# A mixture-of-experts layer that starts its blocks when two of four batches' rows are scattered, not three, with its routing work reordered

## What is computed

```python
x = x + 0.5 * _L0_ffn_ref(_layernorm(x, axis=-1), ln_g, ln_b, router_w, eg, eb, W1, b1, W2, b2, Wo, bo)
x = x + _L0_attn_ref(_layernorm(x, axis=-1), W_qkv, W_o)
x = x + 0.5 * _L0_ffn_ref(_layernorm(x, axis=-1), ln_g, ln_b, router_w, eg, eb, W1, b1, W2, b2, Wo, bo)
```

```python
xf = _layernorm(x.reshape(-1, Dd), ln_g, ln_b)
scores, idx = jax.lax.top_k(xf @ router_w, K)
gate = jax.nn.softmax(scores, axis=-1)
# one expert, for the rows that chose it
x = _layernorm(xf, g, b)
hidden = (x @ W1 + b1) * silu(clip(x @ W2 + b2))
out = out + gate * (hidden @ Wo + bo)
```

## Time and profile before

| | |
|---|---|
| time, median of 3 runs | 1293.15 us (1292.27 to 1294.56) |
| the profiled execution's own time | 1283.73 us |
| its span, and mean granted TensorE clock | 1282.0 us, 0.981 |
| busy: PE, DVE, ACT, POOL | 1144.8, 1124.8, 878.0, 518.6 us |
| the routing, to the first product of the mixture | up to 105 us |
| first mixture, attention, second mixture | from there to about 330, to about 1035, to the end |

### The profile page before, as it was taken

One profiled execution on the slowest core, in us unless ns is written; L12 is line 12 of the kernel. 1 busy time (PEld: TensorE's weight loads), 2 busy tenths in 40 slices (PEclk: granted clock), 3 DMA queues, 4 the chain that ended last, 5 costly groups with the idle time before them and its releaser, 6 DMA issues.

```text
span 1282.0 us, 27027 instructions
## 1 busy us (share of the span) xinstructions
PE 1144.8 (89%) x9003; PEld 606.4 (47%) x9003; DVE 1124.8 (88%) x2287; ACT 878.0 (68%) x1849; POOL 518.6 (40%) x672
## 2 busy tenths in 40 slices
PE   3857999888699999999999999999999999999993
PEld 2745888877322222332223223222222367788882
DVE  7877888887799999989999999999999778988885
ACT  1223555555289999898889888898887965455651
POOL 3883556424224001525336333445344128543232
PEclk9999999999689999999999999999999999999997
DMA  8115565563110200012011000010000413555653
GB/s 278 53 63 181 206 204 194 196 238 137 51 51 18 68 18 4 16 31 55 2 31 37 21 18 18 20 42 10 18 9 25 147 72 142 193 206 191 243 200 141
DMA packets 58746, 123.28 MB, mean 96 GB/s; under 512 B 12736, under 2 KB 33954, under 8 KB 58576
## 3 DMA queue, kind: packets, MB, share of 16 engines
q1 hardware_dynamic: 49616, 103.57, 23.6%
q0 software_dynamic: 8704, 16.93, 4.2%
q10 hardware_dynamic: 288, 1.05, 0.2%
HBM read 36.39 MB, written 23.62 MB: 47 GB/s over the span
## 4 chain that ended last, share of the span: by engine, by line
PE 59%; DVE 25%; POOL 6%; issue 5%; DMA 3%; ACT 2%; SPq 1%; DVEq 0%; POOLq 0%; ACTq 0%
PE psum L2329 15%; DVE att_neg_part L1996 13%; PE psum L2301 9%; PE psum L2232 8%; PE psum L2220 7%; PE psum L2222 7%; PE psum L2283 6%; POOL rows_dram L1293 4%; DVE ffn_x2c L1938 2%; DMA ffn_block_rows<-rows_dram 2%; DVE ffn_hidden L1949 2%; DVE stats L1631 1%; PE psum L2307 1%; ACT ffn_silu L1454 1%; PE psum L2172 1%
## 5 line engine op out<-in xcount | busy, mean ns | idle before, releaser
L1996 DVE TENSOR_REDUCE att_neg_part<-psum 128x2 f32<-128x1024 f32 x512 | 594.7, 1215 | 27.0 <-PE psum L2283 24.9
L1486 ACT ACTIVATE att_probs<-psum 128x512 f32<-128x512 f32 x1024 | 556.4, 597 | 59.8 <-PE psum L2301 23.0
L2329 PE MATMUL psum<-att_probs,att_values 128*18 128x256 f32 x4096 | 322.2, 387 | 4.3 <-issue 3.7
L2283 PE MATMUL psum<-att_right,att_left 62*128 62x512 f16 x1024 | 288.1, 391 | 31.0 <-DVE att_neg_part L1996 30.1
L1454 ACT ACTIVATE ffn_silu<-ffn_x2c,ffn_rec 128x256 f32<-128x256 f32 (+1 forms) x320 | 154.7, 487 | 170.4 <-DVE ffn_x2c L1938 169.9
L1309 POOL DMA_INDIRECT y_dram<-ffn_y,ffn_block_rows x144 | 142.6, 990 | 233.9 <-ACT ffn_y L1472 205.5
L2301 PE MATMUL psum<-att_right,att_left 64*128 64x512 f16 x512 | 199.0, 389 | 0.1
L2307 PE MATMUL psum<-att_right,att_left 64*128 64x512 f16 x512 | 194.9, 381 | 0.0
L1938 DVE TENSOR_SCALAR ffn_x2c<-psum,ffn_rec 128x256 f32<-128x256 f32 (+1 forms) x320 | 162.6, 512 | 34.0 <-PE psum L2222 29.7
L2220 PE MATMUL psum<-ffn_block_t,ffn_rec 128*128 128x256 f32 (+1 forms) x640 | 178.7, 361 | 1.8 <-ACT ffn_block_t L1405 1.8
L2222 PE MATMUL psum<-ffn_block_t,ffn_rec 128*128 128x256 f32 (+1 forms) x640 | 178.0, 360 | 0.0
(11 more groups left out here) (236 smaller groups left out, 1040.8 us busy)
## 6 DMA issues: line engine op xcount, KB each, us to landing
ffn_rec<-record SPq DMA_DIRECT2D x80, 776.5 KB, 3.8
ffn_block_rows<-rows_dram SPq DMA_DIRECT2D x64, 130.0 KB, 3.1
record<-in_L_ffn_W SPq DMA_DIRECT2D x16, 256.0 KB, 6.4
att_left<-q_parts_dram SPq DMA_DIRECT2D x64, 64.0 KB, 2.2
att_right<-att_max_parts SPq DMA_DIRECT2D x256, 1.0 KB
y_dram<-ffn_y,ffn_block_rows POOLq DMA_INDIRECT x144, 2.3
x_sb<-in_L_attn_x SPq DMA_DIRECT2D x4, 512.0 KB, 7.1
record<-in_L_ffn_Wo SPq DMA_DIRECT2D x8, 256.0 KB, 7.2
```

What stands on the lines that cost most here:

```text
L1486: S.activation(probs[:, slot % PROBS, :], ring_bank(("score", slot))[:, :], ACT.Exp, scale=unlift).then_inc(att_bank.by_act, 1)
L1996: V.tensor_reduce(out=neg_part[:, h % 2, keys, p::PAIR, t], in_=psum[:, low:high + 1, :], axis=AX.X, op=ALU.max, negate=True).then_inc(red ...
L2283: product = TE.matmul(bank[max_banks(n)[k]], left[s][PRODUCTS[k], p, q], right[s][PRODUCTS[k], p, seen], start=True, stop=True)
L2329: last = TE.matmul(value_bank[g * VS:g * VS + 2 * VW, p * HALF // 2:(p + 1) * HALF // 2], values_flat[:, at:at + 2 * VW], queries, start=( ...
```

## The change

Six things change, all of them in the first 170 us or so.

1. SP, DVE and ACT start the mixture when the rows of batches 0 and 1 are scattered. The first `AHEAD` = 9 blocks are full ones that two batches fill in any case: `vector_lay_out_early` lists them first, by the new counts `rows_ahead`. SP waits for the rows of batch 2 ahead of block 9. Batch 2's 16 scatters follow behind batch 1's on POOL, and batch 3's 16 all go into `HEAD`.
2. The late layout, nine pieces of DVE work, goes from ahead of the mixture into `HEAD`: one piece ahead of chunk 2 of each of the blocks 2 to 10. SP's eight loads of filler rows move from blocks 8 to 15 to blocks 14 to 16.
3. The rows to be sent out are made by ACT (`scalar_fill`, from a new `offset`), no longer by DVE at step 6. For batch 3 ACT does it in four pieces in `HEAD`, ahead of chunks 1, 2 and 3 of block 1 and chunk 0 of block 2.
4. The list of the routing is written anew: the first norm of a batch (L1660, 8 instructions of DVE) goes from step 0 to step 2, which for batch 1 is behind the places of batch 0; the `fold` passes of PE and ACT go to other places, ACT's behind each batch's exponential and rows.
5. PE may transpose the first half of `xf` when that half is ready, and the PSUM banks of the routing are two shared pairs and no longer one bank for each batch.
6. The scaling of the attention's weights (`scalar_lift`, two instructions of ACT) moves from ahead of the mixture to ahead of chunk 0 of block 3, and the constants of DVE wait for one POOL instruction fewer.

The diff, cut to what the text speaks of (renamed helpers and split semaphores are left out):

```diff
+    AHEAD = -((E * (BLOCK - 1) - TOPK * N * (B - 2)) // BLOCK)
...
-        route_bank = [Banks([bank[b]], semaphore(f"route_full{b}"), semaphore(f"route_emptied{b}"))
-                      for b in range(B)]
+        route_banks = [Banks(bank[2 * k:2 * k + 2], semaphore(f"route_full{k}"), semaphore(f"route_emptied{k}"))
+                       for k in range(2)]
+        route_bank = [route_banks[b % 2] for b in range(B)]
...
-        FIRST_OUT = 2
+        OUT_SLOTS = [0, 2, 4, 6, 8, 10, 12, 14, 16, 18, 20, 24, 28, 32, 36, 40]
         for block in range(BEGIN, BEGIN + 3):
             plan_head(block, [(0, "turned", block, 0)])
-        for n in range(FIRST_OUT, BT * TOPK):
-            HEAD[HC * (n - FIRST_OUT)].append(("route", JOBS[B - 1], ROUTE_STEPS - 1, (n, BT * TOPK)))
+        for n in range(BT * TOPK):
+            HEAD[OUT_SLOTS[n]].append(("route", JOBS[B - 1], ROUTE_STEPS - 1, (n, BT * TOPK)))
+        for n in range(9):
+            HEAD[HC * (1 + n) + 2].append(("lay", 1, 0, (n, 9)))
+        for n in range(4):
+            HEAD[n + 1].append(("fill", B - 1, 0, (n, 4)))
+        HEAD[HC * 2].append(("lift", 0, 0, WHOLE))
...
+            def each(what, pieces):
                 for n in pieces:
-                    if n <= E:
-                        yield "fold", n, 0, WHOLE
+                    yield what, n, 0, WHOLE
+            def scatter(b, places):
+                for n in places:
+                    yield "route", JOBS[b], SCATTER, (n, BT * TOPK)
+            yield "constants", 0, 0, WHOLE
             yield from steps(0, range(6))
             yield from steps(1, (0,))
             yield from steps(0, (6,))
+            yield "fill", 0, 0, (0, 2)
+            yield "fold", 0, 0, WHOLE
+            yield "scale", 0, 0, WHOLE
             yield from steps(1, (1,))
-            yield from steps(0, range(7, SCATTER))
-            yield from folds((0,))
-            for b in range(1, B):
-                yield from steps(b, (2,))
-                yield from folds((3 * b - 2,))
-                yield from scatters(b - 1, 0)
-                yield from steps(b, (3, 4))
-                yield from scatters(b - 1, 1)
-                yield from steps(b, (5,))
-                yield from folds((3 * b - 1, 3 * b))
-                yield from steps(b + 1, (0,))
-                yield from steps(b, (6,))
-                yield from scatters(b - 1, 2)
-                yield from steps(b + 1, (1,))
-                yield from steps(b, (7,))
-                yield from scatters(b - 1, 3)
-                yield from steps(b, (8, 9))
-                if b == B - 1:
-                    yield "folded", 0, 0, WHOLE
-                yield from scatters(b - 1, 4)
-                yield from steps(b, (10, 11))
-                if b == B - 2:
-                    yield "lay", 0, 0, WHOLE
-                yield from scatters(b - 1, 5)
+            yield from steps(0, (7, 8, 9, 10))
+            yield "fill", 0, 0, (1, 2)
+            yield from steps(0, (11,))
+            yield "square", 0, 0, WHOLE
+            yield from each("fold", (1, 2))
+            yield from each("scale", (1, 2))
+            yield from steps(1, (2, 3, 4))
+            yield from scatter(0, range(0, 5))
+            yield from steps(1, (5,))
+            yield "fold", 3, 0, WHOLE
+            yield from steps(2, (0,))
+            yield from steps(1, (7, 8, 9, 6))
+            yield from scatter(0, range(5, 7))
+            yield from each("fold", (4, 5))
+            yield from steps(2, (1,))
+            yield from steps(1, (10,))
+            yield "fill", 1, 0, WHOLE
+            yield from steps(1, (11,))
+            yield from each("scale", (3, 4, 5))
+            yield from scatter(0, range(7, 13))
+            yield from steps(2, (2, 3, 4, 5))
+            yield "fold", 6, 0, WHOLE
+            yield from steps(3, (0,))
+            yield from steps(2, (7, 8, 9, 6))
+            yield from each("fold", (7, 8))
+            yield from scatter(0, range(13, 15))
+            yield from steps(3, (1,))
+            yield from scatter(0, range(15, 16))
+            yield from steps(2, (10,))
+            yield "fill", 2, 0, WHOLE
+            yield from steps(2, (11,))
+            yield from each("scale", (6, 7, 8))
+            yield "lay", 0, 0, WHOLE
+            yield "norm", 0, 0, WHOLE
+            yield "folded", 0, 0, WHOLE
+            yield from scatter(1, range(0, 16))
+            yield from steps(3, (2, 3, 4, 5))
+            yield from steps(3, (7, 8, 9, 6, 10, 11))
+            yield "lifts", 0, 0, WHOLE
+            yield from scatter(2, range(0, 16))
...
-                for job in JOBS[0:B - 1]:
+                for job in JOBS[0:B - 2]:
...
+            if k == 0 and i == AHEAD:
+                sync_rows_written(JOBS[B - 2])
...
-            for n in range(FIRST_OUT):
-                pool_route(JOBS[B - 1], ROUTE_STEPS - 1, (n, BT * TOPK))
...
+                if k_ffn == 0:
+                    G.wait_ge(*rows_by_act(job))
...
+        def scalar_fill(b, part):
+            job, r = JOBS[b], sets[b]
+            S.wait_ge(*by_dve(job, FILLED))
+            for t in share(part, BT):
+                last = S.activation(r.rows[:, t, :, 0:F], r.xf[:, t, :].unsqueeze(1).to_broadcast([P, TOPK, F]),
+                                    ACT.Identity, bias=r.offset[:, t:t + 1], scale=r.rstd[:, t:t + 1])
+            if last_of(part):
+                last.then_inc(r.by_act, 1)
...
-                S.wait_ge(lifts_made, 1)
-                S.activation(wqkv_t[:, :], wqkv_t[:, :], ACT.Copy, scale=lifts[:, 0:1].bitcast(F32))
-                S.activation(wo_t[:, :], wo_t[:, :], ACT.Copy, scale=lifts[:, 1:2].bitcast(F32)).then_inc(lifted, 1)
...
+        def scalar_lift():
+            S.wait_ge(lifts_made, 1)
+            S.activation(wqkv_t[:, :], wqkv_t[:, :], ACT.Copy, scale=lifts[:, 0:1].bitcast(F32))
+            S.activation(wo_t[:, :], wo_t[:, :], ACT.Copy, scale=lifts[:, 1:2].bitcast(F32)).then_inc(lifted, 1)
...
-            vector_lay_out_late()
...
+                    if t == nt // 2 - 1 and k_ffn == 0:
+                        last.then_inc(r.by_dve, 1)
...
+                if k_ffn == 0:
+                    V.scalar_tensor_tensor(r.offset[:, :], r.mean_var[:, :, 0], -1.0, r.rstd[:, :],
+                                           ALU.mult, ALU.mult).then_inc(r.by_dve, 1)
+                    return
...
+            if k_ffn == 0 and b == B - 3:
+                V.tensor_tensor(rows_ahead[:, :], carry[0:1, :], region[0:1, :], ALU.subtract)
...
-                    settle(V.tensor_scalar(firsts_f[:, :], first_rows[:, :], float(BLOCK - 1), None, ALU.add))
-                    settle(V.tensor_copy(firsts_i[:, :], firsts_f[:, :]))
+                    if ahead:
+                        settle(V.tensor_copy(firsts_i[:, :], ahead[:, :]))
+                    else:
+                        settle(V.tensor_scalar(firsts_f[:, :], first_rows[:, :], float(BLOCK - 1), None, ALU.add))
+                        settle(V.tensor_copy(firsts_i[:, :], firsts_f[:, :]))
```

More of the change, by code:

```diff
@@ L304, in build_macaron @@
         powers_i = sbuf("powers_i", [P, 3], I32, first)
-        sets.extend(RouteSet(k, first) for k in range(1, B - 1))
+        sets.extend(RouteSet(k, first) for k in range(1, B - 2))
+        first.close()
+        MIXING = 82 * 256
+        behind = ExitStack()
+        sbuf("before_the_late_set", [P, MIXING], owner=behind)
+        sets.append(RouteSet(B - 2, behind))
+        behind.close()
         sets.append(last_set)
-        first.close()
         class Mixture:
@@ L510, in dve_steps @@
         def dve_steps(job):
-            return [n for n in range(PLACED + 1) if not (on_pool(job) and n in (XF, FILLED))]
+            if job[0] == 0 and job[1]:
+                return [SHIFTED1, XF_FIRST, XF, SHIFTED2, WON, CHOSEN, LED, FILLED, PLACED]
+            return [n for n in range(PLACED + 1) if not (on_pool(job) and n in (XF, FILLED) or job[0] and n == XF_FIRST)]
         def by_dve(job, step):
@@ L1559, in vector_program, with vector_constants @@
         def vector_program():
+            for what, which, step, part in first_routing():
+                if what == "route":
+                    vector_route(which, step, part)
+                elif what == "constants":
+                    vector_constants()
+                elif what == "lay":
+                    vector_lay_out_early(ahead=rows_ahead)
+                elif what == "lifts":
+                    vector_lifts()
+                elif what == "square":
+                    vector_square()
+                elif what == "norm":
+                    vector_norm()
+                elif what == "folded":
+                    vector_fold()
+            vector_experts(0)
+            vector_attention()
+            vector_experts(1)
+            vector_last_sums()
+        def vector_constants():
             V.wait_ge(pool_made, 3)
@@ L1568, in vector_program @@
```

(4 more changed lines are left out.)

107 lines of the change are left out of this document (54 added, 53 removed).

## The result

| | kernel before | changed kernel |
|---|---|---|
| median of 20 runs each | 1295.88 us (1291.14 to 1298.95) | 1298.19 us (1294.80 to 1302.75) |
| ratio, 95% interval | | 1.0020 [1.0011, 1.0029] |
| span of the profiled execution | 1282.0 us | 1293.8 us |

The account below looks back on a forecast made before the run. POOL's scatters were taken to bound the head, PE the mixture. An earlier start, -22.2 us, plus 3.1, 1.0, 0.4 and 0.5 gave -17.2, taken off the median 1293.15: 1276 us, own range 1272 to 1280, over all 1268 to 1285.

Parts of the forecast that it names:

- POOL's wait: Ahead of the mixture: POOL waits about 6 us for DVE before batch 2's second root.
- the root: Batch 2's second root on POOL, ahead of the mixture: DVE has its input ready at 50.0 us.
- the last awaited scatter T: Start of the last of POOL's scatters that the mixture waits for: 76.9 us instead of 99.14.
- layout: First mixture's blocks: late layout's nine DVE pieces, 9.24 us, cost 3.1 beyond the 0.69 free per block; bounds 0 and 5.8.
- rows: First blocks: ACT making batch 3's rows costs 1.0 us, bounds 0 and 3.6.
- scaling: First mixture: ACT's two instructions scaling the weights ahead of a silu cost 0.4 us, bounds 0 and 0.9.
- Filler loads: First mixture: SP's moved loads of filler rows have three blocks of lead, so cost 0.
- batch 3's 4.43 + 2.44: DVE's passes over xf and statistics for batch 3, after the early layout ends at 66; said to end at 73.8.
- slower landings: First mixture: landings slower beside the weights' loads, 0.5 us added.
- "Slower": Rival, chance 0.04: POOL's issues slow down beside DVE and the weights' loads, block 6's rows come late; +13, 1306 us.
- "the blocks up to 10 take over 6.2": Sign of a wrong prediction: first mixture's blocks up to 10 take over 6.2 us; forecast was some 5.9 for blocks 2 to 10.
- the other two: Signs of a wrong prediction: first turn on PE later than 90 us, or PE waiting for rows in blocks 6 to 8.

Follow-up runs that it names:

- e2: The changed kernel, unchanged, profiled again on one chip with the kernel before: 1266.03 us against 1285.31, ratio 0.9844, no stall.
- e1: The kernel before, unchanged, profiled a second time: 1285.15 us, span 1281.6, no stall.
- e11: The changed kernel, unchanged, timed again as the base for other runs where nothing stalled: 1266.85 us, ratio 0.9859 to the kernel before.
- e7: The kernel before, unchanged, profiled on another chip, where it stalled too: 1299.94 us.
- e17: The changed kernel with batch 3's row scatters one a block from block 3 on, in place of two a block up to block 6: 1293.96 us against 1295.38, ratio 0.9994.

## Why the prediction was wrong

**The mechanism and its sizes hold where nothing stalls.** Forecast and measured in e2: first scatter 23.3 and 23.90; POOL's wait 6 and 4.04, the root at 50.0 and 49.78; the last awaited scatter T 76.9 and 77.03; first turn 82.8 and 82.85. From block 0 to 12 the gain over e1 shrinks from 22.1 to 18.7, 3.4 for layout, rows and scaling together, where the terms were 3.1, 1.0 and 0.4. Filler loads, put at 0, cost 1.2 to 1.5 for a time. The span went down by 14.6 (e2) and 16.8 (e11), against e1's, where the sum was 17.2, the medians by 19.3 and 18.4. Executions of before vary by 3 us from run to run and those of the changed kernel in e2 by 6, the profiled one being the longest, so these agree. One slip of the working changes nothing: from 66, batch 3's 4.43 + 2.44 lead to 72.9 and not to 73.8, and its `offset` waits for a root at 79.6 anyway.

**The step that failed** is in the last step of the sum and in its mixture terms: "The profiled execution took 1283.73 in all, 9.4 less than the median 1293.15; the saving is taken off the median". The 9.4 was read as something that stays beside any kernel. It was a different condition: engines stall beside row scatters, in before too, where the head's stalls lie mostly in slack (over 22 us on ACT, 5.8 at the first turn). The sum removed that slack and priced the blocks beside the scatters from a trace without a stall: layout 3.1, rows 1.0, scaling 0.4, slower landings 0.5, in all 5.0 behind the first turn. In the result's profile these blocks pay 26.6 up to block 12 (from 20.7 earlier to 5.9 later than before), 3.4 in e2. In a stalled timing the changed kernel takes 32 to 36 us more than in a quiet one (1298.2 and 1301.8 against 1266.0), before 10 to 15 (1294.9 to 1299.9 against 1285.3).

**Where it went, in the result's own profile against e2** (same program, same instructions): 1.5 us at the first turn, 14.0 at block 3, 22.5 at block 5, 24.8 at block 6, then no more up to block 12. The other 2 to 3 of the 26.8 between the two spans come in the second mixture. A part is TensorE's clock: it is granted 0.78 of full speed from 100 to 130 us and 0.82 from 130 to 150, against 1.00 in e2. Windows of the result's profile (engines' busy time, clock, DMA share, GB/s), then of e2:

```profile
100.00:130.00 30.00, 16.98 (x72) 14.01 (x72) 15.82 (x43) 12.71 (x31) 13.59 (x14) 0.78 0.27 95
130.00:150.00 20.00, 18.09 (x78) 15.67 (x79) 15.35 (x44) 9.55 (x24) 7.85 (x8) 0.82 0.45 164
```

```profile
100.00:130.00 30.00, 29.62 (x146) 25.26 (x145) 27.44 (x85) 17.10 (x45) 22.99 (x24) 1.00 0.61 216
130.00:150.00 20.00, 19.74 (x95) 16.00 (x94) 18.54 (x49) 10.25 (x26) 10.73 (x11) 1.00 0.51 183
```

PE idled for 10 us and the eight products behind it (L2325 at 106.43) took 3.78 at the lower level (1.2 GHz), 1.89 at the full one (at 119.55).

**The rivals.** "Slower" (0.04) had the pair right, POOL's issues beside DVE, and the sides wrong: POOL was to slow down, and keeps 1.26 us an issue while the others stop. The page that was cited with it (the Trainium skill, SBUF — State Buffer, SBUF: two separate sides) is about POOL and DVE on one port; the stalls are on ACT, PE and SP as well, so by this rule they aren't explained. The sign that the prediction was wrong, "the blocks up to 10 take over 6.2", came; the other two didn't.

**Open.** What a stalled engine waits for, and what makes a timing stall. That most long stalls end when POOL pauses fits an engine that is held up for as long as POOL issues back to back, but no run sets the pause by itself. POOL often pauses because it needs what the stalled engine makes (134.88 above), so these profiles can't tell for certain which of the two holds up the other. The scatters' own packets don't show the cause: from an issue's start to its last packet they take 1.9 to 2.1 us in both conditions. Late loads of instructions are a rival that no run tests; the trace has these packets too, and none lands within 2 us of the end of any of the 20 long stalls, which speaks against them.

## What to carry over

A median that lies 9 us above the profiled span is a result to explain before anything is taken off it: profile again until a slow one shows where the time is. Slack hides stalls; a change that removes slack must be priced with the stalls that it uncovers, and timed more than once, on more than one chip. Work beside a queue of indirect DMAs isn't free because a trace once shows it so: here the overlap was worth 24 us in one condition and about 10 in the other.

## What the chip showed beyond that

DVE, ACT, PE and SP stopped for 2 to 11 us with their operands ready, often at the same instructions in different timings, in stretches in which POOL issues row scatters or within 3 us behind them, while POOL kept its pace of 1.26 us. Most of the long ones ended about 2 us behind the last issue of a row. In the kernel before, whose blocks have two result scatters and one row scatter, turns from block 3 to 18 stay 5.62 apart in both conditions (e1, e7); but in e17, with as many from block 3 on, blocks 4 and 5 still took 12.0 and 8.0. And 12 scatters more cost nothing in a quiet timing and, by ratios, 11 us in a stalled one.
